# First attention of a two-layer transformer block: scores computed a second time with keys on partitions, maxima as contraction rows, the future masked by one full-height product per block

## What is computed

```python
b, t, e = x.shape                       # 4, 512, 256
h, d = (H, E // H)                      # 16 heads of 16
Q = (x @ Wq.T).reshape(b, h, t, d)
K = (x @ Wk.T).reshape(b, h, t, d)
V = (x @ Wv.T).reshape(b, h, t, d)
scores = jnp.einsum('bhqd,bhkd->bhqk', Q, K)
causal = jnp.triu(jnp.ones((t, t), bool), k=1)
scores = jnp.where(causal, -jnp.inf, scores)
weights = jax.nn.softmax(scores / jnp.sqrt(jnp.float32(d)), axis=-1)
ctx = jnp.einsum('bhqk,bhkd->bhqd', weights, V)
ctx = ctx.transpose(0, 2, 1, 3).reshape(b, t, e)
return ctx @ Wp.T + bp
```

## Time and profile before

| | us |
|---|---|
| median of 3 runs | 1045.97 (1041.60 to 1046.72) |
| the profiled execution, its own time | 1045.61 |
| its span, first to last instruction | 1043.8 |
| first maximum of the first attention starts | 18.0 |
| last context of the first attention is copied | 314.1 |
| PE busy in the span | 909.4 (87%) |
| DVE busy in the span | 822.5 (79%) |
| ACT busy in the span | 629.8 (60%) |
| POOL busy in the span | 373.0 (36%) |

### The profile page before, as it was taken

How to read it: one execution, slowest core, us unless ns; L and a number is a source line. 1 busy time by engine, 2 the same in 40 slices (tenths; PEclk the granted TensorE clock), 3 DMA queues, 4 the chain that set the end, 5 groups by cost and what they waited for, 6 DMA issues and landing times.

```text
span 1043.8 us, 23337 instructions
## 1 busy us (share of the span) xinstructions
PE 909.4 (87%) x8624; PEld 627.8 (60%) x8745; DVE 822.5 (79%) x2400; ACT 629.8 (60%) x1560; POOL 373.0 (36%) x605
## 2 busy tenths in 40 slices
PE   6778778877767988998899999999999999798796
PEld 3667666766653443434566566666666667586454
DVE  6999998989985787675899988888888888523555
ACT  5999998989862434343666655555555555423443
POOL 4333443430422455444333333333333333200354
PEclk9999999999988999999999999999999999999999
DMA  7202121200000000000466655555565555400011
GB/s 265 63 22 62 42 62 42 56 9 2 2 2 1 1 1 1 1 1 1 77 124 115 123 99 99 99 98 97 100 102 102 102 102 99 91 1 1 1 41 41
DMA packets 174626, 61.41 MB, mean 59 GB/s; under 512 B 169248, under 2 KB 170800, under 8 KB 174384
## 3 DMA queue, kind: packets, MB, share of 16 engines
q1 hardware_dynamic: 174512, 59.90, 28.3%
HBM read 15.83 MB, written 2.10 MB: 17 GB/s over the span
## 4 chain that ended last, share of the span: by engine, by line
PE 50%; DVE 30%; ACT 7%; issue 5%; POOL 5%; DMA 4%; SPq 0%; POOLq 0%; DVEq 0%; ACTq 0%
PE bank L349 12%; PE bank L350 12%; PE bank L348 11%; DVE s_sb L1130 7%; DVE pt_lo L1087 4%; DVE scr L1087 4%; DVE scr L1117 3%; DMA pt_lo<-w_lo 3%; PE bank L663 3%; PE bank L665 3%; PE bank L664 3%; ACT scr L798 2%; ACT s_sb L845 2%; POOL scr L1592 2%; DVE w_lo L1148 2%
## 5 line engine op out<-in xcount | busy, mean ns | idle before, releaser
L1130 DVE CUSTOM_DVE_ANT_0 s_sb<-bank,consts 128x512 f32<-128x512 f32 (+3 forms) x512 | 227.8, 481 | 23.3 <-PE bank L350 15.0
L847 ACT ACTIVATE s_sb<-s_sb,nm 128x512 f32<-128x512 f32 (+3 forms) x256 | 141.5, 553 | 103.7 <-DVE nm L1130 102.4
L348 PE MATMUL bank<-w_hi,scr 128*128 128x256 bf16 (+1 forms) x566 | 169.9, 300 | 16.7 <-DVE scr L1087 13.8
L349 PE MATMUL bank<-w_lo,scr 128*128 128x256 bf16 (+1 forms) x575 | 173.5, 302 | 1.9 <-issue 1.8
L350 PE MATMUL bank<-w_hi,scr 128*128 128x256 bf16 (+1 forms) x572 | 172.0, 301 | 0.1
L798 ACT ACTIVATE scr<-bank 128x256 bf16<-128x256 f32 (+4 forms) x256 | 119.8, 486 | 75.2 <-PE bank L665 43.3
L845 ACT ACTIVATE s_sb<-s_sb,nm 128x512 f32<-128x512 f32 (+3 forms) x256 | 141.0, 583 | 13.3 <-DVE nm L1130 13.2
L1087 DVE TENSOR_TENSOR pt_lo<-bank,pt_hi 128x512 bf16<-128x512 f32 (+1 forms) x192 | 108.5, 592 | 8.1 <-ACT pt_hi L798 8.1
L1622 POOL TENSOR_SCALAR wqkv_hi<-s_sb,rr 128x512 bf16<-128x512 f32 (+3 forms) x128 | 65.6, 532 | 137.6 <-DVE rr L1154 137.6
L1087 DVE TENSOR_TENSOR scr<-bank,scr 128x256 bf16<-128x256 f32 (+1 forms) x160 | 80.5, 524 | 39.6 <-ACT scr L798 39.4
L1622 POOL TENSOR_SCALAR w_hi<-s_sb,rr 128x512 bf16<-128x512 f32 (+3 forms) x128 | 65.6, 532 | 105.2 <-DVE rr L1154 105.2
(11 more groups left out here) (160 smaller groups left out, 2393.7 us busy)
## 6 DMA issues: line engine op xcount, KB each, us to landing
scr<-wall_in SPq DMA_DIRECT2D x19, 512.0 KB, 3.7
x_tok<-x_tok_in SPq DMA_DIRECT2D x1, 2048.0 KB, 10.6
scr<-x_t_in SPq DMA_DIRECT2D x3, 512.0 KB, 9.3
out<-x_tok SPq DMA_DIRECT2D x3, 512.0 KB, 3.1
scr<-wqkv_in SPq DMA_DIRECT2D x2, 384.0 KB, 3.9
pt_hi<-w_hi SPq DMA_TRANSPOSE x32, 3.3
pt_lo<-w_lo SPq DMA_TRANSPOSE x32, 3.4
pt_hi<-wqkv_hi SPq DMA_TRANSPOSE x32, 3.4
```

The lines of the kernel that those rows point to most:

```text
L348: pe.matmul(out, l_hi, r_hi, start=start, stop=False, skip_group_check=check)
L349: pe.matmul(out, l_hi, r_lo, start=False, stop=False, skip_group_check=check)
L847: last = act.activation(at, at, ACT.Exp, bias=nm[:, j % 2, qt:qt + 1], scale=-1.0, accum_out=rs[:, j % 2, qt:qt + 1])
L1130: last = dve.tensor_tensor_reduce(s_sb[j % 2][:, S_OFF[qt]:S_OFF[qt] + w], bank[turn][:, col:col + w], mask[:, 512 - w:512], -scale, HUGE, ...
```

## The change

The heads of the first attention are now worked in 32 pairs (two heads of one group whose rows lie on partitions 0 to 63 and 64 to 127 of the stacks), in `SLOTS` from -6 to 33, and for each pair p:

- `l0_scores` computes the scores with queries on partitions as before, into banks 0 to 2. `l0_maxima` (DVE) runs the same custom instruction, but unscaled and back into the bank; only the negative maxima in `nm0` are used.
- POOL splits these maxima into three bf16 pieces (`l0_split_maxima`, four small instructions that wait for each other), as columns 48 to 50 of `m_cols`.
- `l0_row_maxima` (PE) puts the pair's stacked Q into bank 7 by a product with `ident_b` and adds the turned columns of `m_cols`: so the negative maxima become rows 48 to 50 of `q_max` (copied by ACT). `k_tok` holds ones in the columns that become these rows.
- `l0_turned_scores` (PE) computes the scores a second time with keys on partitions, K's stack by `q_max`, so that the maximum is already subtracted. On each of the four diagonal blocks a product of `ident_b` and `future`, over all 128 partitions, comes first and puts a large negative number where the key lies in the future.
- ACT takes the exponential from the bank straight to `probs` in f32. There is no transposition of probabilities, no `pt_hi` and no `pt_lo`.
- `l0_context` (PE) multiplies 20 blocks of `probs` by 17 columns of V, both f32, in one product each in place of three bf16 ones; ACT copies the 136 columns of a pair.
- V isn't stacked any more: ACT copies it to `v_tok`, SP writes it to `v_by_token` in DRAM and reads it back with 8 positions of each token on partitions (64 bytes a piece).
- `l0_stack` turns 16 pieces for each of two halves of 64 x 64 (32 instructions) into bank 6.
- Every second chunk of `w_hi` is copied by ACT (`weights_high`) instead of POOL, in slots -1 to 25; the bias is added in slots 27 to 30.
- The five early steps stand in the last two slots, 30 and 31, and `small_weights` stands on POOL behind the last of them. PE still waits for `eb_moved` ahead of the loop over `STEPS`.

So the split of each pair's maxima stands in one queue with the large instructions on weights. The core of the diff:

```diff
+            def l0_row_maxima(p):
+                g, j = divmod(p, 2)
+                if g + 2 < NT:
+                    pe.wait_ge(*((a["vt"], g + 3) if j == 1 else (a["plo"], 2 * g + 6)))
+                pe.wait_ge(a["spl"], p + 1)
+                pe.matmul(bank[7][:, :], ident_b[:, :], q_stack[g % 3][:, ds(j * TOK, TOK)], start=True, stop=False,
+                          skip_group_check=True)
+                for qt in range(TT):
+                    last = pe.matmul(bank[7][:, qt * P:(qt + 1) * P], m_cols[p % 2][:, qt, :], ident_b[:, :],
+                                     start=False, stop=True, skip_group_check=True)
+                last.then_inc(a["nm"], 1)
...
+            def l0_turned_scores(p, chunk):
+                g, j = divmod(p, 2)
+                if chunk == 0:
+                    pe.wait_ge(a["qt"], p + 1)
+                out = [bank[3 + (6 * p + 2 * chunk + h) % 3] for h in range(2)]
+                for i, (kt, col) in enumerate(K_CHUNKS[chunk]):
+                    for h in range(2):
+                        if i == 0:
+                            hold(pe, a["exp"], 6 * p + 2 * chunk + h - 2)
+                        pe.matmul(out[h][:, col:col + P], ident_b[:, :], future, start=(i == 0), stop=False,
+                                  skip_group_check=True)
+                    w = TOK - kt * P
+                    for h in range(2):
+                        last = pe.matmul(out[h][:, col:col + w], k_stack[g % 3][half(h), ds(j * TOK + kt * P, P)],
+                                         q_max[p % 2][half(h), kt * P:TOK], start=False, stop=True,
+                                         skip_group_check=True)
+                        if i == len(K_CHUNKS[chunk]) - 1:
+                            last.then_inc(a["st"], 1)
...
+            def l0_context(p):
+                g, j = divmod(p, 2)
+                pe.wait_ge(a["exp"], 6 * p + 6)
+                pe.wait_ge(v_ld[g % 2], 16 * (g // 2 + 1))
+                hold(pe, a["vc"], p)
...
+                            last = pe.matmul(bank[6][:, at:at + VC], probs[p % 2][:, col:col + P],
+                                             v_pos[g % 2][:, 2 * h + j, kt, :], start=(kt == 0), stop=(kt == qt),
+                                             skip_group_check=True)
+            def l0_slot(p):
+                g, j = divmod(p, 2)
+                for chunk in range(3):
+                    if 0 <= p + 2 < NP:
+                        l0_scores(p + 2, chunk)
+                    if 0 <= p < NP:
+                        l0_turned_scores(p, chunk)
+                    if chunk == 0 and 0 <= p + 1 < NP:
+                        l0_row_maxima(p + 1)
+                    if chunk == 1 and 0 <= g + 2 < NT:
+                        l0_stack(g + 2, j)
+                    if chunk == 2 and 0 <= g + 3 < NT:
+                        (l0_project, l0_values)[j](g + 3)
...
+                if 0 <= p - 1 < NP:
+                    l0_context(p - 1)
```

More of the change, by code:

```diff
@@ L1124, in maxima @@
                 hold(dve, s["s"], 3 * u + chunk + 1)
-                if s is c and chunk == 0:
-                    hold(dve, c["tlo"], u - 1)
-                turn = (3 * j + chunk) % (2 if s is a else 4)
+                if chunk == 0:
+                    hold(dve, s["tlo"], u - 1)
+                turn = (3 * j + chunk) % 4
                 for qt, col in S_CHUNKS[chunk]:
```

615 lines of the change are left out of this document (314 added, 301 removed).

## The result

| | before | after |
|---|---|---|
| median, us | 1045.82 (4 runs, 1041.60 to 1046.72) | 1335.87 (4 runs, 1332.67 to 1337.04) |
| span of the profiled execution, us | 1043.8 | 1334.0 |
| last context of the first attention is copied, us | 314.1 | 603.8 |
| mean granted clock of PE | 0.975 | 0.824 |

The ratio is **1.278** (95% interval 1.274 to 1.282), 290 us more, where 1015 us had been forecast with a range up to 1070. The copy of the last context lies 603.8 - 314.1 = 289.7 us later, so all of it lies in the first attention.

A forecast was written before the change was run, and what follows sets the result against it. DVE bounds the kernel before (8.84 us a pair), PE the changed one (7.9 a full slot). Start 21.5, slots 205.4 + 13.8 + 12, early steps 26, end 3 + 3: 284.7 us against 314.1, so 1015, range 960 to 1070.

The follow-up runs named there:

- the probe: The kernel before with plain streams of PE products and DVE copies added behind its last work; 100 float32 products of 17 columns took 39.96 us.
- e2: The changed kernel with one bf16 context product in place of the float32 one, low parts left out, stack copies still slow: 1128.04 us, ratio 1.080.
- e8: The changed kernel with quick-order stack copies, one bf16 context product (low parts left out) and maxima split on DVE instead of POOL: 992.59 us.
- e10: The changed kernel with quick-order stack copies, maxima split on DVE and float32 context products spread in twos behind later score and projection products: 1230.48 us.

## What to carry to other kernels

Price an operation that the trace doesn't show by what it does on its engine (loads, columns, clock), and if the bounds differ by ten times, treat its upper end as a full case and not as a tail. Compare the access pattern of each copy, not its size alone: where one side must jump, let it be the reads, not 2-byte writes 32 bytes apart. And a small job on which a whole pipeline waits doesn't belong on a queue that waits for something unrelated.

## What the runs showed of the hardware

- A float32 product of 128 x 128 weights and 17 columns runs as two loads and two products: 0.20 us in fours at 2.4 GHz, 0.40 in a row at 1.2 GHz; a 16-bit one 0.027 to 0.033. With 128 moving columns it costs 0.22.
- Narrow products in a row take PE's clock to 1.2 GHz though PE never waits (0.57, then 0.50, in the probe). Waits go with a low clock too: e2 and e8 issue the same products, and e2, with its waits for the slow copies, has 0.67 to 0.71 between 100 and 250 us, e8 0.93 and 0.97 between 100 and 200. The 0.138 us behind a wide product in a probe doesn't carry over to a kernel in which the clock is already low (0.33 in e10).
- A bf16 copy from PSUM to SBUF whose neighbours land 32 bytes apart: 4.36 ns an element on DVE, 4.4 to 4.5 on ACT; next to each other 1.2 to 1.4; read in order as well 0.65. Results 4 bytes apart cost 7% more than results side by side.
- Half-height products on the two halves of the rows run at once; a change between half and full height costs 0.10 us.
